# One loop for all sixteen groups of row tiles in a graph aggregation with residual and layer norm

## The reference

```python
def _L0_gnn_ref(X, A_hat, w, W_agg):
    agg = A_hat @ (X @ W_agg)                    # (8192 x 8192) @ (8192 x 64)
    aggregated_term = w[:, None] * relu(agg)
    residual_term = (1.0 - w)[:, None] * X
    return aggregated_term + residual_term
x = _layernorm(x + _L0_gnn_ref(x, adj, w, W_agg), axis=-1)   # eps 1e-5, no scale or shift
```

## Time and profile before

| | us |
|---|---|
| median of 3 runs | 638.62 (638.38 to 640.05) |
| the profiled execution, its own time | 638.89 |
| its span (first to last instruction) | 637.0 |
| PE busy | 519.5 (82%) |
| VectorE busy | 55.8 (9%) |
| ScalarE busy | 15.9 (2%) |
| bytes read from HBM | 270.6 MB, at 428 GB/s over the span |
| mean granted TensorE clock | 0.912 of full |

### The profile page before, as it was taken

One profiled execution on the slowest core, in us unless ns is written; L12 is line 12 of the kernel. 1 busy time (PEld: TensorE's weight loads), 2 busy tenths in 40 slices (PEclk: granted clock), 3 DMA queues, 4 the chain that ended last, 5 costly groups with the idle time before them and its releaser, 6 DMA issues.

```text
span 637.0 us, 5371 instructions
## 1 busy us (share of the span) xinstructions
PE 519.5 (82%) x2304; PEld 177.2 (28%) x2304; DVE 55.8 (9%) x136; ACT 15.9 (2%) x35; POOL 0.3 (0%) x5
## 2 busy tenths in 40 slices
PE   0678798878987888797878977878887987978996
PEld 0123232222222322222222322322222222222345
DVE  2000101010010100101001010100101001010102
ACT  0000000000000000000000000000000000000000
POOL 0000000000000000000000000000000000000000
PEclk9997898888979889897988979898888989888999
DMA  9999999999999999999999999999999999999998
GB/s 362 453 418 453 419 427 433 425 447 428 444 414 447 419 429 443 441 432 419 451 410 436 436 450 423 427 431 425 446 424 453 424 429 419 436 444 420 428 413 349
DMA packets 9667, 272.75 MB, mean 428 GB/s; under 512 B 1472, under 2 KB 1728, under 8 KB 3008
## 3 DMA queue, kind: packets, MB, share of 16 engines
q1 hardware_dynamic: 9360, 272.63, 99.6%
q10 hardware_dynamic: 304, 0.07, 0.1%
HBM read 270.60 MB, written 2.10 MB: 428 GB/s over the span
## 4 chain that ended last, share of the span: by engine, by line
DMA 69%; PE 29%; issue 0%; SPq 0%; ACT 0%; DVE 0%; DVEq 0%
DMA ring<-adj_main_dram 69%; PE bank L156 29%; PE bank L164 0%; SPq L114 0%; ACT aggT L203 0%; ACT aggT L208 0%; SPq L110 0%; SPq L109 0%; DVE res L267 0%; ACT std_last L199 0%; DVE y_last L261 0%; ACT aggT L211 0%; DVE stats L263 0%; DVE y_last L262 0%; DVE mv L264 0%
## 5 line engine op out<-in xcount | busy, mean ns | idle before, releaser
L156 PE MATMUL bank<-ring,x_sb 128*64 128x512 f32 (+2 forms) x2176 | 501.7, 621 | 102.2 <-DMA ring<-adj_main_dram 102.1
L156 PEld LDWEIGHTS bank<-ring,x_sb 128*64 128x64 f32 x2176 | 161.6, 148 | 430.2 <-issue 299.7
L245 DVE SCALAR_TENSOR_TENSOR y<-bank,w_sb 128x256 f32<-128x256 f32 (+1 forms) x16 | 6.7, 420 | 552.7 <-PE bank L164 552.7
L164 PE MATMUL bank<-wagg,aggT 128*128 128x64 f32 x128 | 17.9, 281 | 11.2 <-ACT aggT L203 10.3
L164 PEld LDWEIGHTS bank<-wagg,aggT 128*128 128x128 f32 x128 | 15.6, 191 | 25.4 <-ACT aggT L203 23.5
L203 ACT COPY aggT<-bank 128x512 f32<-128x512 f32 x15 | 8.8, 585 | 527.0 <-PE bank L156 527.0
L234 DVE TENSOR_TENSOR y<-y,res 128x256 f32<-128x256 f32 (+1 forms) x16 | 6.7, 420 | 2.2
L242 DVE TENSOR_TENSOR res<-y,rstd 128x256 f32 (+1 forms) x16 | 6.7, 421 | 0.6
L238 DVE TENSOR_TENSOR sq<-y 128x256 f32<-128x256 f32 (+1 forms) x16 | 6.7, 421 | 0.6
L236 DVE SCALAR_TENSOR_TENSOR y<-rowsum,y 128x256 f32<-128x256 f32 (+1 forms) x16 | 6.7, 420 | 0.5
L239 DVE TENSOR_REDUCE varsum<-sq 128x4 f32<-128x256 f32 (+1 forms) x16 | 6.7, 416 | 0.5
(11 more groups left out here) (9 smaller groups left out, 1.3 us busy)
## 6 DMA issues: line engine op xcount, KB each, us to landing
ring<-adj_main_dram SPq DMA_DIRECT2D x30, 5632.0 KB, 27.2
ring<-adj_main_dram SPq DMA_DIRECT2D x15, 5120.0 KB, 29.8
ring<-adj_mid_dram SPq DMA_DIRECT2D x2, 2304.0 KB, 22.8
ring<-adj_mid_dram SPq DMA_DIRECT2D x1, 3072.0 KB, 21.5
ring<-adj_mid_dram SPq DMA_DIRECT2D x2, 1536.0 KB, 23.9
x_sb<-x_dram SPq DMA_DIRECT2D x1, 2048.0 KB, 8.0
out_dram<-res SPq DMA_DIRECT2D x1, 2016.0 KB, 8.1
ring<-adj_last_dram SPq DMA_DIRECT2D x2, 768.0 KB, 23.0
```

Source lines behind the costliest of these rows:

```text
L156: last = nc.tensor.matmul(into[j % 2 * D:(j % 2 + 1) * D, 0:cols], x_sb[:, j], ring[:, at + s * cols:at + (s + 1) * cols], start=j < 2, st ...
L164: last = nc.tensor.matmul(rows[:, i * D:(i + 1) * D], aggT[:, i * P:(i + 1) * P], wagg2[:], start=True, stop=True)
L245: step(nc.vector.scalar_tensor_tensor(out=y[:, 0:n], in0=rows.rearrange("p (n d) -> p n d", d=D), scalar=0.0, in1=over_row(w_sb[:, bass.ds ...
```

## The change

There are now sixteen groups of four row tiles and no others. On every compute engine one loop runs over all 16. The host still hands over three arrays (14 main groups, one "mid", one "last", each of 4 row tiles now), since SP issues them differently: the main ones in its loop, the mid one with the same three loads in straight code, and the last one in pieces: each of the three loads is cut, in (12, 10), (12, 10) and (7, 5, 3, 2, 2, 1) slots. TensorE's loop has a wait before each piece. For pieces after the first of a load that wait is on a semaphore of its own, which GpSimd sets to one at the start (seven small memsets); the value waited for is 1 in groups 0 to 14 and 17 in group 15, from `(g + 1) // G * 16 + 1`. ScalarE copies the sum in four copies of 128 columns, and TensorE turns each back as soon as it is copied. The special code for mid and last groups is gone, with the short chain of VectorE. SP now stores row tiles 0 to 59, ScalarE the last 4. The waits on x_in and wagg_in moved into TensorE's loop, and the second PSUM bank is the only one for rows.

```diff
-MAIN_LOADS = (22, 22, 20)
-MID_LOADS = (16, 12, 12, 8, 8, 4, 2, 2)
-LAST_LOADS = (10, 12, 12, 10, 7, 5, 4, 2, 2)
+LAST_PIECES = ((12, 10), (12, 10), (7, 5, 3, 2, 2, 1))
...
+            for c in range(C):
+                sp.wait_ge(slot_free, MAIN * C + (c + 1 - C))
+                load(c, adj_mid[0:1])
             j = 0
+            for c, pieces in enumerate(LAST_PIECES):
+                sp.wait_ge(slot_free, (MAIN + 1) * C + (c + 1 - C))
+                at = c * SLOT
+                for k, n in enumerate(pieces):
+                    sp.dma_start(ring[:, at:at + n * COLS], adj_last[:, j:j + n].rearrange("q s n -> q (s n)")
+                                 ).then_inc(piece_loaded[c][k - 1] if k else loaded[c], 16)
+                    j, at = j + n, at + n * COLS
+
+            sp.wait_ge(out_ready, G - 1)
             sp.dma_start(out_rows[:, 0:LAST_T0], res[:, 0:LAST_T0]).then_inc(stored, 16)
...
             nc.gpsimd.memset(eps[:], EPS).then_inc(eps_ready, 1)
+            for k, piece in enumerate(sum(piece_loaded, [])):
+
+                nc.gpsimd.memset(ones[:, k:k + 1], 1.0).then_inc(piece, 1)
...
+            with pe.Fori(0, G) as g:
+                pe.wait_ge(x_in, 16)
+                pe.wait_ge(wagg_in, 32)
+                j = 0
+                for c, pieces in enumerate(LAST_PIECES):
+                    pe.wait_ge(loaded[c], g * 16 + 16)
+                    at = c * SLOT
+                    for k, n in enumerate(pieces):
+                        if k:
+
+                            pe.wait_ge(piece_loaded[c][k - 1], (g + 1) // G * 16 + 1)
+                        last = contract(at, j, n)
+                        j, at = j + n, at + n * COLS
+                    last.then_inc(slot_free, 1)
+
+                pe.wait_ge(dve_step, g * DVE_GROUP + DVE_PRE)
+                for i in range(MAIN_SLOTS):
+                    pe.wait_ge(agg_copied, g * MAIN_SLOTS + (i + 1))
+                    last = nc.tensor.matmul(rows_ps[:, i * D:(i + 1) * D], aggT[:, i * P:(i + 1) * P], wagg2[:], start=True, stop=True)
                 last.then_inc(rows_done, 1)
...
             with act.Fori(0, G) as g:
                 act.wait_ge(slot_free, g * C + C)
-                nc.scalar.copy(aggT[:], acc).then_inc(agg_copied, 1)
-                std_of(std[:], varsum[:], 1.0 / D, g * DVE_GROUP + (DVE_PRE + VAR_STEP))
+                for i in range(MAIN_SLOTS):
+                    nc.scalar.copy(aggT[:, i * P:(i + 1) * P], acc[:, i * P:(i + 1) * P]).then_inc(agg_copied, 1)
+                act.wait_ge(dve_step, g * DVE_GROUP + (DVE_PRE + VAR_STEP))
+                nc.scalar.activation(std[:], varsum[:], ACT.Sqrt, bias=eps[:, 0:1], scale=1.0 / D).then_inc(std_ready, 1)
...
-            v, t = y_last[:], LAST_T0
-            dve.wait_ge(rows_done, LAST + 1)
-            step(nc.vector.tensor_scalar(v, last_rows, 0.0, w_sb[:, t:t + 1], ALU.max, ALU.mult), LAST_STEP0 + 1)
-            step(nc.vector.tensor_tensor(v, v, res[:, t], ALU.add), LAST_STEP0 + 2)
-            step(nc.vector.bn_stats(stats[:], v), LAST_STEP0 + 3)
-            step(nc.vector.bn_aggr(mv[:], stats[:]), LAST_STEP0 + LAST_VAR_STEP)
-            dve.wait_ge(std_ready, LAST + 1)
-            step(nc.vector.reciprocal(rstd_last[:], std_last[:]), LAST_STEP0 + 5)
-            nc.vector.tensor_scalar(res[:, t], v, mv[:, 0:1], rstd_last[:, 0:1], ALU.subtract, ALU.mult).then_inc(out_ready, 1)
```

More of the change, by code:

```diff
@@ L34, in gnn_residual_layernorm @@
     T = x.shape[0] // P
[L35 to L44, removed]
+    MAIN = adj_main.shape[0]
+    G = MAIN + 2
+    LAST_T0 = T - LAST_SLOTS
+    COLS = MAIN_SLOTS * P
+    LOADS = [sum(pieces) for pieces in LAST_PIECES]
+    C = len(LOADS)
+    SLOT = max(LOADS) * COLS
+    assert SUB == T == sum(LOADS) and G * MAIN_SLOTS == T == 64
+    assert MID_SLOTS == LAST_SLOTS == MAIN_SLOTS
     DVE_PRE = 2
     DVE_GROUP, VAR_STEP = 7, 6
-    LAST_STEP0 = DVE_PRE + LAST * DVE_GROUP
-    LAST_VAR_STEP = 4
     ctx = ExitStack()
@@ L69, in gnn_residual_layernorm @@
         eps = sb("eps", [P, 1])
+        ones = sb("ones", [P, sum(len(pieces) - 1 for pieces in LAST_PIECES)])
         aggT = sb("aggT", [P, COLS])
@@ L110, in _, with load @@
             sp.dma_start(w_sb[:], w.rearrange("(p t) -> p t", p=P)).then_inc(w_in, 16)
-            def main_load(c, load):
-                j, n = sum(MAIN_LOADS[:c]), MAIN_LOADS[c]
-                sp.dma_start(ring[:, c * SLOT:c * SLOT + n * COLS], load[:, :, j:j + n].rearrange("o q s n -> (o q) (s n)")
+            def load(c, group):
+                j, n = sum(LOADS[:c]), LOADS[c]
+                sp.dma_start(ring[:, c * SLOT:c * SLOT + n * COLS], group[:, :, j:j + n].rearrange("o q s n -> (o q) (s n)")
@@ L115, in main_load @@
                              ).then_inc(loaded[c], 16)
             for c in range(C):
-                main_load(c, adj_main[0:1, 0])
-            with sp.Fori(1, G) as g:
+                load(c, adj_main[0:1, 0])
+            with sp.Fori(1, MAIN) as g:
                 for c in range(C):
                     sp.wait_ge(slot_free, g * C + (c + 1 - C))
[L123 to L132, removed]
@@ L133, in _ @@
-            sp.wait_ge(slot_free, G * C)
-            j = 0
[L135 to L140, removed]
+                    load(c, adj_main[bass.ds(g, 1), 0])
+            for c in range(C):
+                sp.wait_ge(slot_free, MAIN * C + (c + 1 - C))
+                load(c, adj_mid[0:1])
@@ L160, in turn_back @@
[L160 to L164, removed]
-                last.then_inc(rows_done, 1)
[L167 to L185, removed]
@@ L186, in _ @@
-            last.then_inc(last_done, 1)
-            turn_back(last_rows, LAST_SLOTS, LAST + 1)
+                    last = nc.tensor.matmul(acc[j % 2 * D:(j % 2 + 1) * D], x_sb[:, j],
+                                            ring[:, at + s * COLS:at + (s + 1) * COLS], start=j < 2, stop=j >= T - 2)
+                return last
+            with pe.Fori(0, G) as g:
[15 more added lines that the diff above has]
+                    last = nc.tensor.matmul(rows_ps[:, i * D:(i + 1) * D], aggT[:, i * P:(i + 1) * P], wagg2[:], start=True, stop=True)
+                last.then_inc(rows_done, 1)
@@ L271 @@
+                dve.wait_ge(std_ready, g + 1)
+                step(nc.vector.reciprocal(rstd[:], std[:]), base + DVE_GROUP)
+                nc.vector.tensor_tensor(residual, y[:], over_row(rstd[:]), ALU.mult).then_inc(out_ready, 1)
 def kernel(x, adj, L0_gnn_w, L0_gnn_W_agg):
```

65 lines of the change are left out of this document (15 added, 50 removed).

## The result

The changed kernel takes 642.06 us (median of 5, 641.81 to 642.20), the kernel before 638.88 in the same session (638.38 to 640.05). The ratio is 1.0043, with a 95% interval of 1.0031 to 1.0054: 3.2 us or 0.4% slower. The profiled execution took 642.11, its span is 640.3.

A forecast was written before the change was run, and what follows sets the result against it. The load stream bounds the kernel up to 591.91, then the tail counts fully. 631.75 + 1.08 + 0.50 + 0.15 + 3.89 + 0.16 = 637.53, plus store 1.9 and 0.4, gives span 639.85 (+2.85); median 641.5, range 639.7 to 643.4.

The forecast's parts named there:

- Up to 591.91, nothing: Through group 14's last landing: added waits, register steps and copies stay hidden behind the load stream, landing stays at 591.91.
- Last landing 631.15: End of the stream: ten pieces, 7 extra loads at 0.065 each, last landing at 631.15, a gain of 0.45.
- TensorE's end 0.6 after it: Group 15: TensorE keeps up with the pieces and ends its last slot at 631.75, 0.4 earlier than before.
- My list: Group 15's forecast piece arrivals, about 599.2 to 631.15, and when TensorE works each off, second pair by 631.4.
- rival 2: TensorE's clock falls in the last group, costing up to 1.7 in the last load: 643.2; chance 10%.
- Copies 1.08, turning back 0.50: After TensorE's last slot: four copies in a row take 1.08, three turnings back lie under them, the last costs 0.50.
- 0.15 and 3.89 on VectorE, 0.16 to the issue, 1.9 for the store: Tail after turning back: gap 0.15, VectorE's chain 3.89, ScalarE's loop 0.16 to the store's issue, its four-tile store 1.9.
- SP's store no longer matters: SP's store, ready at about 607 but queued behind the loads, ends at 635.7, before ScalarE's at 639.45.
- Rival 1: First lap's instruction packet, which makes one DMA engine 1.46 late, is gone: 640.05, not slower; chance 20%.
- Rival 3: The loop's code is fetched again each lap, 15 or more instruction packets: 663, or 643 to 644; chance 3%.

The follow-up runs named there:

- experiment 5: The changed kernel with the last group in three whole loads, no pieces and no piece semaphores: 649.72 us (1.0166).
- experiments 3 and 4: The changed kernel with its last load cut (7, 5, 3, 2, 1, 1, 1) and (7, 5, 4, 2, 2): 641.84 and 641.92 us.
- experiment 1: The changed kernel with group 15 as straight code outside the loops of TensorE, ScalarE and VectorE: 641.90 us (1.0040).
- end_ones: The changed kernel with last pieces (7, 5, 3, 2, 1, 1, 1) instead of (7, 5, 3, 2, 2, 1): 641.84 us (1.0041).
- experiment 12: The kernel before, unchanged, for a second profile and more runs: 638.88 us in 12 runs (1.0000).
- experiment 8: The changed kernel with a first empty pass of TensorE over its code before any data is there: 642.09 us (1.0047).

## Why the prediction was right

The mechanism, its place and all terms of the sum but one held. Span 639.85 forecast, 640.3 measured.

- **Up to 591.91, nothing:** 591.78. The seven waits, the register steps and the copies are hidden.
- **Last landing 631.15:** 631.07. Seven loads cost 0.5 (experiment 5), forecast 0.45.
- **TensorE's end 0.6 after it:** 1.35. This is the term that was mis-sized, by 0.7: TensorE ended 0.3 later than before (632.42 against 632.14), not 0.4 earlier. I took 0.44 as the time of a slot; it is the mean of two slots abreast, each of which takes 0.86 on its half, plus the longer end of the last matmul (experiments 3 and 4). My list didn't give the 0.6 either: with the second pair done at 631.4, a last slot of 0.44 ends at 631.84, not 631.75.
- **The clock** (rival 2). It fell in group 14's last load, not in the last group: 40 matmuls in 10.50 us at a granted clock of 0.84 (partly at 1.2 GHz), and 1.00 (2.4 GHz) from 603.8 on. The next windows show it, columns as in the earlier trace rows. The first pieces of group 15 were late by 1.3 for it and the end was not, as experiment 1 confirms. The gaps before were 0.84 and 2.45, and it fell behind the longer one, as I had read it in the earlier trace rows. But the length of a gap doesn't decide it: in the trace of end_ones the clock stayed at 1.00 behind gaps of 3.66 and 2.46, and in experiment 12's it fell behind one of 1.19 (44 matmuls from 566.25 on took 11.36 us). What decides it is open; my rival had three gaps of one lap to go by.

```profile
579.70:589.40 9.70, 9.66 (x44) 3.07 (x44) 0.00 (x0) 0.00 (x0) 0.00 (x0) 1.00 0.95 408
591.80:602.40 10.60, 10.50 (x40) 3.18 (x40) 0.00 (x0) 0.03 (x1) 0.00 (x0) 0.84 0.98 418
603.80:632.40 28.60, 28.55 (x128) 10.17 (x128) 3.14 (x8) 0.30 (x1) 0.00 (x0) 1.00 1.01 424
```

The two loads in end_ones:

```profile
579.51 9.66 PE L135 MATMUL bank<-ring,x_sb 128*64 128x512 f32 x44 [3.66 <-DMA ring<-adj_mid_dram]
591.63 8.80 PE L135 MATMUL bank<-ring,x_sb 128*64 128x512 f32 x40 [2.46 <-DMA ring<-adj_mid_dram]
```

- **Copies 1.08, turning back 0.50:** together 1.46 instead of 1.58. The copies do overlap, four in 0.77 us, 0.29 less than 4 x 0.265. The Trainium skill ("ScalarE: Activation LUTs", section "What ACT_TABLE_LOAD costs") gives about 93 ns for each overlap of back-to-back ACTIVATEs, 0.28 for three, and these copies agree with it. What I missed is that the turning back then is the longer one, 1.12 from the first copy on, so only 0.12 of the 0.29 arrived.
- **0.15 and 3.89 on VectorE, 0.16 to the issue, 1.9 for the store:** 633.88 to 634.01, 3.88, 0.17, 1.85.
- **SP's store no longer matters:** landed at 635.6, forecast 635.7.
- **Rival 1** had the right cause and the wrong outlook. The first packet came in the first lap as before, and one was left of three. The two that went had cost next to nothing: the 39.7 us from 591.91 to the last landing of before are what 38.78 and 14 extra loads at 0.07 make, 39.8.
- **Rival 3:** one packet in the span; the loop's code is not fetched again.

The misses partly cancel, which is luck. The 0.75 at TensorE's end, less 0.08 of an earlier landing, 0.12 of copies and turning back and 0.1 of small terms, is the 0.45 by which the span was longer than forecast; the last 0.1 to the measured median lies outside the span.

## What to carry to other kernels

Find what runs after the last byte, and what else is still running by then: a store queued behind the loads is free as long as the engines' tail is longer than it (here 4.6 us of store), and a last group whose tail is shorter than that would gain nothing more, as I read it. Merging small last groups into the regular loop added nothing in the laps here and put the work of each further row tile behind the last byte, 1.2 to 1.3 us each. When a rate is a mean over units that run abreast, it says nothing about the last unit: time that one from start to end.

## What the hardware showed that I had not expected

- With one instruction packet of 16 KB a load of a full stream lands 1.0 to 1.5 us late: 13.13 us behind the load before in the changed kernel and 13.59 in the earlier trace rows, instead of 12.13, and the first load at 23.71 instead of 22.37 in experiment 8. Nothing of it is made up: from the third load of the first lap to that of group 14 it is 14 laps of 38.8 us in each of the three traces. That one of 16 DMA engines falls behind is not shown.
- Two matmul sequences on the two halves of TensorE's columns run beside each other: 0.43 us from start to start on each half, and 0.59 for the last.
- Four independent copies of 265 to 298 ns start 0.16 us apart on ScalarE, 0.77 us for all.
